# Six full expert tiles before the last batch is finished, and all weight loads on the sync queue

## The reference

```python
# layer 1, x: [8, 512, 256], 16 heads of 16
q, k, v = split(x @ Wqkv);  q, k = rope(q), rope(k)
q, k = q / norm(q), k / norm(k)
a = softmax(q @ k.T / 4) @ v
x = ln(x + a @ Wo + bo)
# layer 2
h = ln_w(x, ln1_w, ln1_b)
y = x + softmax(q2 @ k2.T / 4) @ v2 @ w_proj      # q2, k2, v2 from h @ w_qkv
z = ln_w(y, ln2_w, ln2_b)
e = argmax(z @ gate_w + gate_b)                   # one of 8 experts per token
m = gelu(z @ w1[e]) @ w2[e]                       # 256 -> 1024 -> 256
out = ln(x + y + m)
```

## Time and profile before

| | |
|---|---|
| median of 3 runs | 1380.87 us (1378.91 to 1381.5) |
| profiled execution | 1376.04 us, its span 1374.0 us |
| PE busy | 1256.9 us, 91% of the span |
| ACT busy | 915.8 us, 67% |
| DVE busy | 793.3 us, 58% |
| POOL busy | 323.5 us, 24% |
| mean granted TensorE clock | 0.97 of full speed |

### The profile page before, as it was taken

One profiled execution on the slowest core, in us unless ns is written; L12 is line 12 of the kernel. 1 busy time (PEld: TensorE's weight loads), 2 busy tenths in 40 slices (PEclk: granted clock), 3 DMA queues, 4 the chain that ended last, 5 costly groups with the idle time before them and its releaser, 6 DMA issues. The chain is left out here.

```text
span 1374.0 us, 20853 instructions
## 1 busy us (share of the span) xinstructions
PE 1256.9 (91%) x7142; PEld 674.2 (49%) x7142; DVE 793.3 (58%) x1815; ACT 915.8 (67%) x1617; POOL 323.5 (24%) x246
## 2 busy tenths in 40 slices
PE   4699999999998898999999999999982899999996
PEld 2233343343343333444444444444332799999986
DVE  5236456456451777787878787878744234443432
ACT  1588878878876575676766666666661477776765
POOL 3113332332331111022222222222123012212211
PEclk8899999999999899999999999999996899999998
DMA  5173243243243121214131313131349211111110
GB/s 180 64 170 105 72 139 98 71 141 95 73 137 108 47 90 50 79 47 109 47 109 47 109 47 109 48 93 47 126 153 311 71 56 51 54 56 51 58 52 15
DMA packets 101485, 123.11 MB, mean 90 GB/s; under 512 B 7234, under 2 KB 87234, under 8 KB 101379
## 3 DMA queue, kind: packets, MB, share of 16 engines
q1 hardware_dynamic: 76534, 83.35, 19.6%
q10 hardware_dynamic: 20416, 25.56, 5.9%
q0 software_dynamic: 4432, 12.87, 3.1%
HBM read 47.41 MB, written 24.27 MB: 52 GB/s over the span
## 5 line engine op out<-in xcount | busy, mean ns | idle before, releaser
L692 ACT ACTIVATE w_space<-bank 128x512 f32<-128x512 f32 x1024 | 561.7, 606 | 277.7 <-PE bank L472 263.6
L886 DVE TENSOR_REDUCE negm<-bank 128x1 f32<-128x512 f32 x512 | 334.3, 685 | 97.9 <-PE bank L504 94.4
L472 PE MATMUL bank<-w_space 96*128 96x512 bf16 (+1 forms) x1024 | 355.1, 385 | 26.5 <-DMA w_space<-work_space 14.2
L489 PE MATMUL bank<-w_space 128*32 128x512 f32 x2048 | 275.3, 610 | 0.2 <-ACT w_space L701 0.2
L472 PEld LDWEIGHTS bank<-w_space 96*128 96x128 bf16 (+1 forms) x1024 | 93.5, 99 | 303.7 <-ACT w_space L692 217.3
L504 PE MATMUL bank<-w_space 96*128 96x512 bf16 x512 | 197.5, 386 | 18.1 <-DVE negm L886 8.8
L666 PE MATMUL bank<-w_space,work_space 128*128 x624 | 141.2, 380 | 0.0
L535 PE MATMUL bank<-work_space,wqkv_sb 128*128 128x512 f32 x256 | 125.0, 613 | 9.5 <-DMA wqkv_sb<-in_w_qkv_dram 6.4
L1245 POOL TENSOR_TENSOR work_space<-w_space,work_space 128x1024 bf16<-128x1024 f32 x32 | 68.3, 2133 | 266.3 <-ACT work_space L742 146.5
L666 PEld LDWEIGHTS bank<-w_space,work_space 128*128 128x128 f32 x624 | 115.6, 190 | 14.3
L1300 POOL DMA_INDIRECT out_dram<-rows_sb,work_space x39 | 59.8, 1533 | 241.9 <-DVE rows_sb L1197 241.9
(11 more groups left out here) (130 smaller groups left out, 1414.3 us busy)
## 6 DMA issues: line engine op xcount, KB each, us to landing
w_space<-work_space SPq DMA_DIRECT2D x372, 128.0 KB
w_space<-in_w_dram SPq DMA_DIRECT2D x10, 1024.0 KB, 14.2
work_space<-rows_dram SPq DMA_DIRECT2D x39, 256.5 KB, 2.6
w_space<-in_w_dram ACTq DMA_DIRECT2D x6, 1024.0 KB, 6.3
work_space<-in_x_t_dram ACTq DMA_DIRECT2D x8, 512.0 KB, 3.7
work_space<-in_x_dram ACTq DMA_DIRECT2D x8, 512.0 KB
x_dram<-xo SPq DMA_DIRECT2D x16, 256.0 KB, 4.2
h_dram<-row_sb SPq DMA_DIRECT2D x16, 256.0 KB, 2.2
```

The lines of the kernel that those rows point to most:

```text
L472: nc.tensor.matmul(bank[:, :], k_stack[0:rows, b % 2, HEADS_AT_ONCE * g + j, kt * P:(kt + 1) * P], q_stack[0:rows, b % 2, HEADS_AT_ONCE * ...
L489: last = nc.tensor.matmul(pv_bank[VW * j:VW * (j + 1), :], v_aug[:, b % 2, at:at + VW], probs[:, q % PROBS, j, :], start=(kt == 0), stop=( ...
L692: nc.scalar.activation(probs[:, q % PROBS, j, :], st_bank(b, c)[0][:, :], ACT.Exp, scale=SCALE).then_inc(exps, 1)
L886: ve.tensor_reduce(negm[:, c % TT, c // TT:c // TT + 1], mx_ring.bank(b, (g, c))[:, :], axis=AX.X, op=ALU.max, negate=True).then_inc(mx_ri ...
```

## The change

**Six early tiles.** After the attention of six of the eight layer-2 batches an expert's list has some whole multiples of 128 rows that no later row can alter. `early_table` counts these, cuts them in tiles, and writes expert and first row of the first six. It stands at quad 12 of stage 16, ahead of the counting of batch 14. The table of the other 33 is made later in two pieces, `late_experts` and `late_rows`, which leave the early tiles out.

**A new order at the end.** The stage loops end one stage sooner, and `tasks` leaves out batch 15's `FINISHED`. These tasks are written out by hand between the steps of tiles 0 to 2 on TensorE, ACT and DVE. They use one PSUM bank of their own, 7. `R2` of batch 15 is done for each half of the batch. The inverse roots of tiles 0 and 1 come behind the gelu of tile 2. TensorE now waits for all of w2 before the first down and for the late table before the expert of tile 6.

**Weight loads.** All 16 are issued by SP: seven when batch 14 has been scored and summed, w1 of 2 and 6 at half of batch 15's scores, then the row loads of the six early tiles, then w1 of 3 and 7 and the last five of w2. The values of the second layer change places (`1 - b % 2`), and the turned rows of its batches go over the rotation tables (`turned_late`), so that those weights find room.

**Weight and bias of the norms.** POOL's two steps are gone. The rows are stored without them, and where they lie turned, with a channel on a partition, scale and bias are applied by the copy out of PSUM: ACT's copies of `T0`, `T1` and `HT` (in two pieces) and DVE's copy of a tile's rows (in two pieces). `ln_t` brings them in one small DMA in place of four.

**Six row buffers.** `ROWS_AHEAD` is 6, and the work space is larger.

```diff
-ROWS_AHEAD = 4
+ROWS_AHEAD = 6
+EARLY = ROWS_AHEAD
+LATE = TILES - EARLY
...
-            if b is not None:
+            if b is not None and (b, places) != (LAST, FINISHED):
...
-        for n in range(-1, STAGES + 1):
+        for n in range(-1, STAGES):
...
+        for name in ("TO3", "TP0", "TP1", "WO0", "WO1", "HT0", "HT1", "GT0", "GT1", "RT"):
+            o_ring.add(LAST, name, 1)
...
@@ TensorE
-            pe.wait_ge(tiles_ready, 1)
-            pe.wait_ge(weights_in[1], 16 * E)
+            pe.wait_ge(early_ready, 1)
...
             transpose_in(0)
-            up(0)
+            task("TO3", LAST)
+            up(0, (0,))
+            task("TP0", LAST)
+            task("TP1", LAST)
             transpose_in(1)
-            for j in range(1, TILES):
+            up(0, (1,))
+            task("WO0", LAST)
+            task("WO1", LAST)
+            up(1)
+            task("HT0", LAST)
+            task("HT1", LAST)
+            transpose_in(2)
+            task("GT0", LAST)
+            task("GT1", LAST)
+            up(2, (0,))
+            task("RT", LAST)
+            up(2, (1,))
+            pe.wait_ge(weights_in[1], 16 * E)
+            down(0, expert_of(0))
+            transpose_in(3)
+            down(1, expert_of(1))
+            for j in range(3, TILES):
+                if j - 1 == EARLY:
+                    pe.wait_ge(tiles_ready, 1)
                 e = expert_of(j - 1)
                 up(j)
...
@@ ACT
-                if n == last + 1 and q in (3, 7, 11):
-                    which, experts = {3: (0, (0, 1)), 7: (0, (4, 5)), 11: (1, (6, 7))}[q]
-                    load_weights(act, which, experts, [(scores, CHUNKS * last),
-                                                       (parts_ready, 2 * last + 2)])
...
-            gelu(0)
-            for j in range(1, TILES):
+            task("TP0", LAST)
+            gelu(0, (0,))
+            task("TP1", LAST)
+            task("R20", LAST)
+            task("R21", LAST)
+            gelu(0, (1,))
+            gelu(1)
+            task("HT0", LAST)
+            task("HT1", LAST)
+            gelu(2)
+            last_norm(0)
+            last_norm(1)
+            for j in range(3, TILES):
                 gelu(j)
                 last_norm(j - 1)
...
@@ DVE
+                    if (n, q) == (LAST + 1, QUADS - 4):
+                        early_table()
...
             def tile_in(j):
                 dve.wait_ge(xs_T, j + 1)
-                ve.tensor_copy(xsT[:, j % 2, :, :].rearrange("p k t -> p (k t)"),
-                               psum[4][:, 0:D]).then_inc(xsT_ready, 1)
+                for k in range(KD):
+                    ve.tensor_scalar(xsT[:, j % 2, k, :], psum[4][:, k * P:(k + 1) * P],
+                                     ln_sb[:, 1, 0, k:k + 1], ln_sb[:, 1, 1, k:k + 1],
+                                     ALU.mult, ALU.add).then_inc(xsT_ready, 1)
...
-            dve.wait_ge(tiles_ready, 2)
+            dve.wait_ge(early_ready, 2)
+            tile_in(0)
             dve.wait_ge(weights_in[0], 16 * E)
             weights_of(0)
-            tile_in(0)
+            task("TO3", LAST)
             weights_of(1)
             tile_in(1)
-            for j in range(1, TILES):
-                if j > 1:
-                    tile_out(j - 2)
+            for name in ("WO0", "M0", "WO1", "M1", "N20", "N21"):
+                task(name, LAST)
+            weights_of(2)
+            tile_in(2)
+            task("GT0", LAST)
+            task("GT1", LAST)
+            weights_of(3)
+            task("RT", LAST)
+            tile_in(3)
+            tile_sum(0)
+            tile_out(0)
+            tile_sum(1)
+            late_experts()
+            for j in range(3, TILES):
+                tile_out(j - 2)
+                if j + 1 == EARLY:
+                    dve.wait_ge(tiles_ready, 2)
                 if j + 1 < TILES:
                     weights_of(j + 1)
                     tile_in(j + 1)
                 tile_sum(j - 1)
+                if j == 3:
+                    late_rows()
...
@@ SP
-            load_weights(sp, 0, (2, 3, 6, 7), [(scores, CHUNKS * (last + 1)),
-                                               (dispatched, 16 * TT * (BATCH - 1))])
-            load_weights(sp, 1, (0, 1, 2, 3, 4), [(pv_done, QUADS * (last + 1))])
-            load_weights(sp, 1, (5,), [o_ring.full(last, "GT1")])
+            load_weights(sp, 0, (0, 1, 4, 5), [(scores, CHUNKS * LAST)])
+            load_weights(sp, 1, (6, 7), [(parts_ready, 2 * LAST + 2)])
+            load_weights(sp, 1, (5,), [(pv_done, QUADS * LAST)])
+            load_weights(sp, 0, (2, 6), [(scores, CHUNKS * LAST + CHUNKS // 2)])
...
+            sp.wait_ge(early_ready, 2)
+            sp.wait_ge(dispatched, 16 * TT * (BATCH - 2))
+            for j in range(EARLY):
+                load_tile(j)
+            load_weights(sp, 0, (3, 7), [(scores, CHUNKS * (LAST + 1))])
+            for slot in range(PROBS):
+                load_weights(sp, 1, (slot,), [(pv_done, QUADS * (LAST + 1) + slot + 1 - PROBS)])
+            load_weights(sp, 1, (PROBS,), [o_ring.full(LAST, "TO3")])
             sp.wait_ge(tiles_ready, 2)
             sp.wait_ge(dispatched, 16 * TT * BATCH)
-            for j in range(TILES):
+            for j in range(EARLY, TILES):
                 load_tile(j)
```

More of the change, by code:

```diff
@@ L631, in _ @@
                             task(name, b)
-            pe.wait_ge(tiles_ready, 1)
-            pe.wait_ge(weights_in[1], 16 * E)
+            for c in range(2):
+                pe.wait_ge(*mx_ring.empty(LAST, (GROUPS - 1, HEADS_AT_ONCE * TT - 1 - c)))
+            pe.wait_ge(early_ready, 1)
             def transpose_in(j):
                 pe.wait_ge(rows_arrived[j % ROWS_AHEAD], 16 * (j // ROWS_AHEAD) + 16)
-                wait(pe, xsT_ready, j)
+                wait(pe, xsT_ready, KD * j)
                 for k in range(KD):
@@ L643, in transpose_in, with up @@
                 last.then_inc(xs_T, 1)
-            def up(j):
-                pe.wait_ge(xsT_ready, j + 1)
+            def up(j, halves=(0, 1)):
+                pe.wait_ge(xsT_ready, KD * j + KD)
                 pe.wait_ge(w1_ready, j + 1)
-                for n in range(2):
+                for n in halves:
                     wait(pe, gelu_done, 2 * j + (n - 3))
@@ L703, in task @@
             def task(name, b):
-                kind, u = name[:2], int(name[-1]) if name[-1].isdigit() else 0
+                kind, u = name[:2], int(name[-1]) if name[-1].isdigit() and name not in ("R1", "R2") else 0
                 p, o = p_ring, o_ring
@@ L707, in task @@
                     act.wait_ge(*p.full(b, name))
-                    nc.scalar.activation(xT[:, u, :], p.bank(b, name)[:, :], ACT.Copy
+                    nc.scalar.activation(xT[:, u, :], p.bank(b, name)[:, :], ACT.Identity,
+                                         scale=ln_sb[:, 0, 0, u:u + 1], bias=ln_sb[:, 0, 1, u:u + 1]
                                          ).then_inc(p.drain_sem(b, name), 1)
@@ L837, in _, with gelu @@
                             task(name, b)
-            def gelu(j):
-                for n in range(2):
+            def gelu(j, halves=(0, 1)):
+                for n in halves:
                     act.wait_ge(up_done, 2 * j + (n + 1))
@@ L1292, in _ @@
                             task(name, b)
+            for name in ("WO0", "WO1", "RT"):
+                task(name, LAST)
             for j in range(TILES):
```

253 lines of the change are left out of this document (160 added, 93 removed).

## The result

| | before | after |
|---|---|---|
| median of 4 runs | 1380.36 us (1378.91 to 1381.5) | 1362.36 us (1360.85 to 1363.73) |
| ratio | | 0.9871, 95% interval 0.9859 to 0.9882 |
| profiled execution, its span | 1376.04, 1374.0 us | 1363.73, 1361.9 us |
| POOL busy | 323.5 us | 239.9 us |

The kernel is 18.0 us faster; 26 were forecast. The time lies in the predicted range (1346 to 1365) and 1.4 us above the forecast case's own (1349 to 1361). The two traces differ by 12.1 us only, since the profiled run of before lies 4.3 us under its median and that of after 1.4 above.

The account below looks back on a forecast made before the run. TensorE bounds attention and experts; the winnable hole is the idle chain of batch 15 between them. 23.0 us to the mark + 4.4 row waits - 1.3 late table = 26.1 us off the median 1380.87: forecast 1355, range 1346 to 1365.

Parts of the forecast that it names:

- forecast case: The prediction's main case for the whole kernel: 1355 us, own range 1349 to 1361, given 62 in 100.
- step 1: Early tiles' table on DVE, quad 12 of batch 15's attention: some 4 us of small steps, costed at zero, at most 2.
- later first tile: Rival, 16 in 100: w1 pair lands after 14.2 us, or clock stays at 1.2 GHz; one gives 1361, both 1366.
- Step 2: Last w1 pair (experts 3 and 7), issued near the last value products: lands after 8.6 us, at 1031.5.
- Step 3: Before the first up: lookup 0.32 and DVE's weight copy 1.23 us, done at 1033.1; first half of up(0) takes 3.7.
- Steps 4 to 6: Batch 15's finishing around up(0) and up(1): up(0) through at 1040.7, up(1) at 1048.7, ACT free for HT1 at 1053.0.
- Step 7: From HT1 through the gate and up(2): done at 1062.2, with the clock back at 2.4 GHz.
- 8, mark: Three tiles through the first product, two through the second: reached at 1069.4 instead of 1092.36, 23.0 us earlier.
- The strips: Seven megabytes of weights streaming beside batch 15's strips of maxima: 0 to 3 us lost, taken as 0.
- The pieces for HT: ACT's copy of the turned rows in pieces: about 0.1 us added each, hidden.
- Behind the mark: Remaining tile loop: 4.4 us of row waits won by six buffers, 1.3 us lost to the late table.
- POOL's removed work: Scale and shift taken off POOL, two steps of about 1.3 us per half: zero, perhaps 3 us won.

## Why the prediction was right, and where it was not

The order of things came as predicted: work of the first tiles between the steps of batch 15, idle before the first tile, ended by DVE's weight copy, which waits for a load; a second pause of 3.8 us before `HT1` (about 4 predicted), ended by ACT; no wait for w2 before the first down; no waits for rows; a period near 7.25 us, so the two DVE steps per tile fit. The early table cost nothing (step 1): no wait of TensorE there names it. The sizes were off, and the time is the one that the rival *later first tile* gave (1361 for one of its two halves), each of its halves having come about in part. One of the signs of being wrong came true as well: the attention of batch 15 ends 9 us later than before (1033.97 against 1024.95), 5.5 us by the strip's stretch and 4.5 by the late start of this execution, less 1.0 won between. Against PV end:

| step | predicted | measured |
|---|---|---|
| 2, pair landed | 6.6 us | 10.2 us |
| 3, first up starts | 8.2 | 12.7 |
| 4, up(0) through | 15.8 | 19.8 |
| 5, up(1) through | 23.8 | 27.8 |
| 6, first half turned, `HT1` | 28.1 | 32.3 |
| 7, up(2) through | 37.3 | 44.2 |
| 8, mark | 44.5 | 51.3 |

- **Step 2 failed by 3.7 us.** I priced the pair at 8.6 us, "nearer to the first, since the pair stands ahead of the five w2 loads in its queue". It took 12.06. Standing ahead did not spare it: w2 cost 1.2 us and the scatter 2.35. The residual took about 1.3, by what is left over. By itself the pair took 7.22, near the 7.9 of my sum. My own sum over what shares, pair, scatter and residual at 357 GB/s, gave 10.3 us and was nearer than the value that I took; it lacked w2. Step 3's copy came 0.8 us later than its terms say.
- **Steps 4 to 6 held.** 19.6 us from the first up to `HT1` against 19.9. ACT's loads cost 1.28 us each and nothing more. After the change:

```profile
1060.88 1.28 ACT L832 ACT_TABLE_LOAD   x1
1062.17 0.20 ACT L832 ACTIVATE rstd<-rstd 128x2 f32<-128x2 f32 x1
```

  The Exp starts 0.01 us after its load. The Trainium skill ("ScalarE: Activation LUTs", section "What ACT_TABLE_LOAD costs") adds a drain of 1.38 us to a switch; the trace does not agree here either.
- **Step 7 failed by 2.7 us.** "I let the clock be back at 2.4 GHz by then": it had been back (granted clock 1.00 from 1050.0 to 1061.9), and it fell again. The pause of 3.8 us before `HT1` lies between, and behind it the granted clock was 0.53 up to 1076. That this pause alone did it isn't shown: with the pair alone two pauses of 1.7 and 1.9 us stood there, and the clock fell to 0.50 too. The gate, which I took as cold once, took 1.88 us twice, and half of up(2) 3.76 where the whole takes 3.73 at full clock:

```profile
1070.16 1.88 PE L616 MATMUL bank<-gate_w_sb,sin_sb 128*128 128x8 f32 x8 [0.27 <-DVE logits L1156]
1071.89 3.76 PE L673 MATMUL bank<-work_space,wqkv_sb 128*128 128x128 f32 x16
```

- **The strips were not free.** "0 to 3 us lost, I take 0" was 4.6 of wait and about 2 at the lower clock. SP had begun its seven loads of 1 MB at 967.61, five were issued and the sixth was being issued, when ACT issued the strip at 978.77.
- **The pieces for HT** cost 1.03 us for two, against 0.60 for the plain copy before (0.80 for one piece with scale and bias): 0.2 each, not 0.1, and not hidden in layer 2.
- **Behind the mark** 5.0 us were won against 3.1: the 4.4 of row waits as predicted, shown by putting them back. The late table, priced at 1.3, shows in the one wait of 0.5 us, at the tile behind it (a period of 8.0 us for 7.25).
- **POOL's removed work** won 2.4 us at the stage between the layers by the traces, inside "perhaps 3 us won".

From the forecast's 26.1 us: less 6.85 to the mark, 5.5 for the strip's stretch and 1.4 for the other stages, plus 2.4 and 1.9, makes 16.7; the medians say 18.0, the traces 12.1 with the late start of one of them (16.7 less 4.5). The 1.3 us between 16.7 and 18.0 are open. That the time lies in the range is in part luck: the three losses alone, 13.75 us on top of 1354.8, would have put it near 1368.5, above the range, and the 4.3 us won that the sum did not count brought it back.

## What to carry to other kernels

When a chain is pulled apart to overlap it with other work, write down each load in flight at that moment and let them share the bytes; a place ahead in one queue did not protect the pair here, neither from the other queues (2.35 us for the scatter) nor from the loads behind it (1.2 us). Put the work whose inputs are there ahead of a wait for a load on an in-order engine, not behind it: here that brought the ratio from 0.9871 to 0.9821. Each wait taken away uncovers the next (w1, then the residual, then the scatter), so look for what lands just before the one that is blamed.

## What the runs showed of the hardware

- A strip of 12 KB issued beside 1 MB loads made TensorE wait 4.6 us, and the granted clock was then 0.51 for 4.9 us (products of 0.61 for 0.38 us each), a loss of about 2 us more.
- A pair of 1 MB loads took 7.22 us by itself, 9.71 with a load of 0.5 MB beside it and 5 MB behind it in its own queue, 10.86 with the 0.5 MB and a scatter of 1.05 MB beside it, and 12.06 with all of them.
- Behind the pause of 11.2 us the granted clock was 0.55 for 3.4 us, about 1.2 GHz: the first 16 matmuls took 3.46 us where 32 take 3.73 at full clock. From 1066.2 us on, behind the pause of 3.8 us, it was 0.53 for 9.8 us. Both stretches cost TensorE time on top of the pauses.
- Two pieces of 128x256 on ACT took 0.59 us each as a mean and 1.03 together, one of 128x512 0.80 (both with scale and bias), 0.60 without.
